# A decoder layer on one core: VectorE adds the negated maxima of 6 of 32 score tiles, 13 warm-up products, and all orders written anew

## What is computed

```python
# 1. linear attention, 16 heads of depth 8
q = elu(x @ Wq + bq) + 1 ; k = elu(x @ Wk + bk) + 1 ; v = x @ Wv + bv
k = k / sqrt(sum(k * k) + EPS)
attn = (q k^T) v @ Wo + bo
x = layernorm(x + (layernorm(x + attn) * gamma + beta))
# 2. cross attention to 64 context rows, 16 heads of 64
scores = (x @ Wq) (ctx @ Wk)^T / 8
out = softmax(scores) (ctx @ Wv) @ Wo
x = layernorm(x + out)
# 3. gated MLP, every operand rounded to FP4 in blocks of 16
h = silu(fp4(x) @ fp4(w_gate)^T) * (fp4(x) @ fp4(w_up)^T)      # 352 wide
x = layernorm(x + fp4(h) @ fp4(w_down)^T)
```

## Time and profile before

| | |
|---|---|
| median of 3 runs | 372.65 us |
| profiled execution, its own time | 374.35 us |
| its span | 372.6 us |
| PE, DVE, ACT, POOL busy | 351.0, 307.9, 253.4, 269.1 us |
| PE weight loads busy | 268.7 us |
| DMA | 10.44 MB, mean 28 GB/s |

### The profile page before, as it was taken

How to read it: one execution, slowest core, us unless ns; L and a number is a source line. 1 busy time by engine, 2 the same in 40 slices (tenths; PEclk the granted TensorE clock), 3 DMA queues, 4 the chain that set the end, 5 groups by cost and what they waited for, 6 DMA issues and landing times.

```text
span 372.6 us, 7321 instructions
## 1 busy us (share of the span) xinstructions
PE 351.0 (94%) x2143; PEld 268.7 (72%) x2143; DVE 307.9 (83%) x858; ACT 253.4 (68%) x533; POOL 269.1 (72%) x453
## 2 busy tenths in 40 slices
PE   7999998999998999999999999999999999998874
PEld 6688655775775968778678867786777788887663
DVE  2798756658689998869989779979998998999994
ACT  2757867586677678668687767868767656864553
POOL 4403549967988689969779895898989569784535
PEclk9999999999999999999999999999999999999998
DMA  7900100001000001000000000000000000000010
GB/s 251 300 2 16 30 1 14 16 16 29 15 17 14 2 15 43 16 30 17 15 29 14 17 1 17 28 3 0 17 15 2 15 2 0 8 23 14 3 30 28
DMA packets 13586, 10.44 MB, mean 28 GB/s; under 512 B 971, under 2 KB 12396, under 8 KB 13548
## 3 DMA queue, kind: packets, MB, share of 16 engines
q1 hardware_dynamic: 12540, 7.89, 7.0%
q10 hardware_dynamic: 1008, 2.10, 1.7%
HBM read 7.88 MB, written 2.10 MB: 27 GB/s over the span
## 4 chain that ended last, share of the span: by engine, by line
PE 71%; POOL 8%; DVE 8%; issue 6%; ACT 5%; DMA 1%; POOLq 0%; ACTq 0%; DVEq 0%
PE A L2860 13%; PE S L2833 12%; PE TP L2823 7%; PE F L2879 6%; PE TP L2851 6%; PE A L2895 5%; PE A L2784 3%; PE S L2842 3%; PE TP L2762 2%; POOL pe L431 2%; PE S L2762 2%; PE F L2762 2%; PE TP L2888 2%; PE A L2797 2%; DMA wqkT<-in_wk_t 1%
## 5 line engine op out<-in xcount | busy, mean ns | idle before, releaser
L431 POOL TENSOR_TENSOR pe<-pe,srec 128x1024 f32<-128x1024 f32 x32 | 60.9, 1904 | 9.2 <-DVE srec L1835 8.9
L2833 PE MATMUL S<-M,x1T 128*128 128x512 f32 x128 | 60.7, 597 | 1.5 <-ACT pe L1064 1.4
L2860 PEld LDWEIGHTS A<-wvoT,wqkT 128*128 128x128 f32 x480 | 56.4, 192 | 3.1 <-issue 1.8
L2860 PE MATMUL A<-wvoT,wqkT 128*128 128x128 f32 x480 | 58.0, 276 | 0.1
L425 POOL TENSOR_TENSOR fold<-pe 128x512 f32<-128x512 f32 x32 | 40.8, 1276 | 14.5 <-ACT pe L1064 14.2
L1818 DVE TENSOR_REDUCE smax<-S 128x16 fp32r<-128x1024 f32 x32 | 38.7, 1210 | 3.2 <-PE S L2833 3.1
L1064 ACT ACTIVATE pe<-S 128x1024 f32<-128x1024 f32 x32 | 32.6, 1020 | 10.6 <-PE S L2842 10.3
L1069 ACT ACTIVATE wqkT<-TP 128x1024 f32<-128x1024 f32 x32 | 32.6, 1019 | 4.3 <-PE TP L2851 4.1
L2833 PEld LDWEIGHTS S<-M,x1T 128*128 128x128 f32 x128 | 22.2, 190 | 18.3 <-issue 15.3
L2879 PE MATMUL F<-w_gu_r,xf_r 128*128 128x352 f32 x168 | 35.0, 344 | 0.1
L2851 PE MATMUL TP<-ident,pe 128*128 128x128 f32 x256 | 33.5, 274 | 1.6 <-POOL pe L431 1.0
(11 more groups left out here) (247 smaller groups left out, 890.2 us busy)
## 6 DMA issues: line engine op xcount, KB each, us to landing
xT<-in_x_t SPq DMA_DIRECT2D x16, 128.0 KB, 2.1
x_sb<-in_x SPq DMA_DIRECT2D x16, 128.0 KB, 2.1
out<-yf SPq DMA_DIRECT2D x15, 128.0 KB, 1.8
M<-in_fw SPq DMA_DIRECT2D x1, 560.0 KB, 11.0
wqkT<-in_wq_t ACTq DMA_DIRECT2D x2, 256.0 KB, 4.5
wqkT<-in_wk_t ACTq DMA_DIRECT2D x2, 256.0 KB, 5.8
ctx_f<-in_ctx_t ACTq DMA_DIRECT2D x2, 256.0 KB, 6.9
wvoT<-in_wv_t ACTq DMA_DIRECT2D x1, 512.0 KB, 9.2
```

The costliest lines, as they stand in the source:

```text
L431: ge.tensor_tensor(w, w, spread(srec[n % 2][:, :], HX, R), ALU.mult).then_inc(pn_made, 1)
L2833: last = te.matmul(S[:, half * BANK:half * BANK + BANK], x1T[b % 2][:, t * P:t * P + P], M[:, b // BH, HC * half:HC * half + HC, b % BH * ...
L2860: last = te.matmul(A2[:, t * P:t * P + P], pT[n % 2][:, j, :], vo[b % 2][:, j, :], start=(j == 0), stop=(j == NJ - 1))
```

## The change

There are four parts.

1. In the lists, `scores_shift` of tiles (1,1), (3,1), (5,1), (7,1), (9,1) and (11,1) stands in DVE's list and no longer in PE's. On DVE it is one addition of 128x1024 in place in PSUM.
2. `WARM` goes from 8 to 13, and the second group of `keep_warm` near the end from 14 to 19. The first of those two groups keeps its 7 products, writes to `F0` in place of `TP0` and stands one `gate_up` earlier.
3. All five lists are in a new order, SP's too.
4. Storage: `xf_r` lies in the tile `GT`, which is free once `m_product` is done; `xfT` has two buffers; the number of `fold`, `ssum` and `srec` buffers has a name (`NFO`), and it is 2 as before. New branches (`SUM_ON_PE`, `WHOLE_GATE`, `TILE_SUM_ON_PE`) are switched off: the sets are empty and the flag is False.

```diff
-        NXB, NA, NPE = 4, 5, 3
+        NXB, NA, NPE, NFO = 4, 5, 3, 2
...
-        xf_r = several("xf_r", 2, [P, 2, T * P], FP32R)
-        xfT = sb("xfT", [P, T * P])
+
+        xf_r = [GT[:, k, 0:2 * T, :].rearrange("p (s t) n -> p s (t n)", s=2) for k in range(2)]
+        xfT = several("xfT", 2, [P, T * P])
...
+        WHOLE_GATE = ()
+
+        SUM_ON_PE = ()
+
+        TILE_SUM_ON_PE = False
...
-        WARM = 8
+        WARM = 13
...
-                wait_free(pool, ssum_made, n - 1)
+                wait_free(pool, ssum_made, n - NFO + 1)
...
+                if b in SUM_ON_PE:
+                    pe.wait_ge(x1_made, T * b + T)
+                    te.matmul(part(A2, t), ident[:, :], x1[b % NA][:, t, :], start=True, stop=False)
...
```

More of the change, by code:

```diff
@@ L2875, in gate_up @@
                 pe.wait_ge(xfT_kept, b + 1)
+                if b in WHOLE_GATE:
+                    for m, bk in enumerate(ffn_banks(b)):
+                        last = te.matmul(bk[:, 0:I], part(xfT[b % 2], t), w_gu[:, m, :], start=True, stop=True)
+                    last.then_inc(gu_made, 1)
+                    return
                 pe.wait_ge(xf_low_made, b + 1)
@@ L3216, in _ @@
             pe.wait_ge(yx_made, 5)
+            down(0)
+            pe.wait_ge(vo_kept, 7)
+            p_transpose(5, 1)
+            pe.wait_ge(yf_made, 1)
             down(1)
@@ L3250, in _ @@
-            p_transpose(6, 0)
+            pe.wait_ge(h_made, 7)
+            gate_up(3, 1)
+            pe.wait_ge(fk_made, 11)
+            project_q(9)
             pe.wait_ge(ya_made, 9)
             kv_outer(9)
-            pe.wait_ge(h_made, 7)
-            gate_up(3, 1)
+            pe.wait_ge(pT_kept, 13)
+            p_transpose(6, 1)
+            kv_project(9)
+            pe.wait_ge(fq_made, 10)
+            down(2)
+            attn_out(9)
+            pe.wait_ge(yf_made, 3)
+            cross_out(6, 0)
@@ new lines, in _ @@
+            pe.wait_ge(yx_made, 9)
+            project_kv(13)
+            pe.wait_ge(pe_made, 20)
+            x1_transpose(10)
+            pe.wait_ge(pT_kept, 19)
+            values(10)
+            pe.wait_ge(fk_made, 14)
+            xf_transpose(6)
+            pe.wait_ge(x1T_kept, 11)
+            scores(10, 0)
+            pe.wait_ge(ky_made, 39)
+            kv_project(11)
+            pe.wait_ge(vo_kept, 11)
+            h_transpose(5)
+            pe.wait_ge(kvo_kept, 12)
+            kv_outer(12)
@@ L3381, in _ @@
+            pe.wait_ge(yf_made, 6)
+            xf_transpose(7)
+            pe.wait_ge(vo_kept, 12)
+            h_transpose(6)
+            pe.wait_ge(xf_low_made, 8)
+            project_q(11)
+            pe.wait_ge(hT_kept, 7)
+            p_transpose(10, 0)
+            pe.wait_ge(hg4_made, 7)
+            gate_up(7, 0)
+            pe.wait_ge(fq_made, 12)
+            down(6)
+            pe.wait_ge(ky_made, 42)
+            attn_out(11)
+            pe.wait_ge(yf_made, 7)
             project_q(12)
-            pe.wait_ge(xg_made, 9)
@@ new lines, in _ @@
+            xf_transpose(10)
+            pe.wait_ge(xg_made, 11)
+            kv_outer(15)
+            pe.wait_ge(hT_kept, 10)
+            values(14)
+            pe.wait_ge(xf_low_made, 11)
+            down(9)
+            pe.wait_ge(xg_made, 12)
+            kv_project(15)
+            pe.wait_ge(hg4_made, 10)
+            gate_up(10, 0)
+            attn_out(15)
+            pe.wait_ge(yf_made, 10)
+            xf_transpose(11)
+            pe.wait_ge(pe_made, 28)
+            x1_transpose(14)
```

2800 lines of the change are left out of this document (1393 added, 1407 removed).

## The result

The changed kernel takes 376.66 us (median of 4, 376.47 to 376.84) and the kernel before, run beside it, 372.65 us (372.3 to 372.77): ratio 1.0109, 95% interval 1.0092 to 1.0127. It is slower by 4.0 us; 369.4 was predicted, and the range ended at 374.5.

What follows compares the result with a forecast made beforehand. PE's list was taken to bound some 310 us, DVE's remaining work and the last tile's chain a 43 us tail. -3.1 + 1.2 - 1.4 + 0.3 - 0.3 = -3.3 from 374.35, less 1.70: 369.4 us, range 365.5 to 374.5.

Steps and rivals of the forecast that it cites:

- Six shifts off PE: Long stretch: six shifts at 0.51 us leave PE's list, -3.1 us (at most 4.1).
- six additions on DVE: Six tiles: 1.21 us each on DVE, S free 0.7 us later; 30% of 4.1 us taken, +1.2 us.
- The cover: Score tiles: PE's other products hide most of the later release of S; 30% of 4.1 us stays uncovered.
- the first rival: Long stretch: PE waits for all 7.3 us of added DVE work; +2.8 us, 375.5 us; chance 0.18.
- Work moved past the last scores: Ahead of scores(15, 1) PE has 1.4 us less work, so the last tile starts 1.4 us sooner: -1.4 us.
- The prediction's own mark: Long stretch, 120 to 320 us: the prediction is wrong if PE's idle time grows past 6 us.
- The third rival: 53.6 to 120 us: the new order also closes half of PE's 5.2 us idle time; 366.8 us; chance 0.18.
- The tail: After the last score maximum: later transposes, less DVE work after the last residual; +0.3 us, length stays 43 us.
- The warm-up and the start: Start: thirteen products close the gap before the weights, first products run at full clock; -0.3 us (-1.5 to +0.9).
- At nothing: Parts priced at zero: five more products near the end (0.12 us each), the storage changes, SP's list with store_out(2).
- DVE sets the pace: Long stretch: DVE goes to 92% busy and PE waits for all 7.3 us added; 375.5 us; chance 0.18.
- The score tile's path eats it: Score tiles: all 4.1 us of the later release of S fall on PE; no change, 372.3 us; chance 0.12.

Runs made afterwards that it cites:

- 13-product run: The kernel before with 13 warm-up products at the start in place of 8, nothing else: 372.56 us, ratio to before 0.9967.
- the filled wait: Changed kernel without its first tail warm-up group (375.1 us), with p_transpose(7,0) moved ahead of x1_transpose(8), which waited 1.35 us: 376.33 us.
- the one experiment on the rest of the tail: Changed kernel without its first tail warm-up group, with down(13) moved behind tile_gate_up(15,0) on PE alone: 377.69 us.
- the run with the new start: Changed lists up to tile (1,1), its shift on PE, 13 warm-up products and the new storage, then the lists of the kernel before: 373.39 us.
- the short sums: score_sums reads half its columns, in both orders: 376.68 us in the changed kernel, 373.86 in the kernel before (beside its 373.93).

## Why the prediction failed, step by step

*Six shifts off PE, and six additions on DVE* (-3.1 and +1.2): right, in the changed order. The addition was sized at 1.21 us and took 1.218. Together -1.9 us, measured -1.9; only the sum was measured. The cover was not the one that I named, though. I took 30% from PE's few waits; in the old order the same additions lose 4.3 us between the first maximum and the last, where -1.9 would have been a gain, so there the additions cost 4.3 + 3.1 = 7.4 us by my price of the shifts, the whole of their 7.3. That is the first rival's arithmetic, but not its reason: taking 6.4 us of other work off DVE gives nothing. What an addition delays is awaited, `S` at (3,1), a small result at (5,1) and (7,1), and only an order laid around it hides it.

*Work moved past the last scores* (-1.4): this is the step that failed. I counted PE's products ahead of the last `scores` and took for granted that the new order runs as tightly as the old one. With the shifts on PE the last maximum comes 2.6 us later than in the 13-product run, where I had it 1.4 earlier: 4.0 us off. The prediction's own mark was passed, PE's idle time in the long stretch went from 1.9 to 6.5 us. The named waits there are for `A` and `S`; that closing one doesn't help was shown once (the filled wait). But little of the 4.0 us is idle time: from 20 to 328 us it is 6.9 us with the shifts back on PE and 7.2 in the 13-product run. One can add up, for both traces and up to the last `scores`, the time from the start of each PE step to the start of the next, less the recorded idle time (an estimate, good to a few tenths, since some product rows are missing from a trace). What I had counted is there: `cross_out` and `h_transpose` take 3.1 us less and `gate_up` 1.6 more, together -1.5 where I had -1.4. But the same calls of `attn_out` take 1.3 us more, `down` and `scores` 0.8 each and `x1_transpose` 0.6, 3.6 us in all, to which 0.7 us of recorded idle time up to that point come; the changed kernel's trace shows the same four within 0.3 us. So the step that failed is the price of the calls that stayed: I put their change at nothing. Whether a call takes longer because of a short wait that the profile counts as busy or because of its new neighbours, no run separates.

The third rival's premise came true and more: between 53.6 and 120 us PE's idle time fell by 4.1 us of 5.2. The last maximum is late all the same.

*The tail* (+0.3, bounds -1.5 and +1.5): mis-sized, 3.0 us against the 13-product run, and past the 1.5 us that I had named as a mark too. I read the moved calls and never priced the first warm-up group at its new place: 1.6 us, shown by taking it out. The other 1.5 us lie on DVE between `h_max(14)` and `h_scaled(14)`, by the traces. I had DVE's list of the tail as a sum of work on either side of the last tile's residual, and not as an order of steps in front of sequence 14's rounding, on which the end waits. That is read and not tested, since the one experiment on the rest of the tail was confounded.

*The warm-up and the start* (-0.3): of little weight, and of a wrong frame. The 1.16 us product and the earlier third `m_product` (14.07, where I had 14.6) came as forecast, but I priced them against an execution with the low-clock start and then took off 1.70 us for the median, which already has the good start. Counted against the lower group the start brings nothing: the same order in front of the old lists is 0.8 us above the 13-product kernel (0.4 in the spans).

*At nothing*: of the five products at the end this holds by the trace. `h_transpose(14)` still waits 0.28 us for POOL behind the group, so the group is covered; only their size was wrong, since 19 products take 4.40 us, 0.23 each and not 0.12. The storage and the place of `store_out(2)` are in the run with the new start as well, and cost there, together with that start, 0.8 us at most. They were not tried singly.

The sum in measured terms: order 2.6, tail 2.9 to 3.0, additions -1.9, together 3.7 in the trace (374.9 - 371.2), 4.0 to 4.1 in the medians. Of the 7.3 us between 369.4 and 376.66, 4.0 are the order up to the last scores, 2.7 the tail, and 0.3 the gain of the start that the median already had; the last 0.3 lie between traces and medians. Of the rivals, *DVE sets the pace* came nearest in its number (375.5), by luck, since the loss has other terms. As a mechanism the short sums speak against it, and against the rule beside it: by the Trainium skill, Perfetto Trace Analysis, "Identifying the Most-Contended Engine", an engine's busy share tells how contended it is, and PE's headroom is judged by its weight loads. By these DVE at 84% against weight loads at 72% is the most contended engine; the trace has these shares, but 6.4 us less on that engine changed nothing. *The score tile's path eats it* was the mechanism of part of the old order's loss (the 1.76 us at (3,1)); in the new order the additions win 1.9 us over the shifts, so it isn't the reason there.

## What to carry to other kernels

Moving work between engines and reordering the lists are two changes, and each needs its own price: run the order without the move and the move without the order. The price of a step on an in-order engine is set by who awaits what stands behind it, not by the engine's busy share; a count of the calls ahead of a mark says when it could come, not when it does. Before a trace is used as the base of a sum, look whether its start is that of the median run.

## What the chip showed that I had not expected

Eight warm-up products followed by a gap before the weights are there don't fix the level at which the first real products run: in the old order they take 2.08 us in three traces (gaps of 1.29 to 1.34 us) and 1.16 in a fourth (1.15 us), and the run times of before part by some 1.4 us. In the new order a gap of 0.90 us gave 2.08 as well, so the length of the gap alone doesn't decide it. With thirteen products `g_product(0)` took 1.16 us in the traces of the 13-product kernel and of the changed one, and at most 1.27 in any other. In the tail a wait of 1.6 us on PE was followed by a granted clock of 0.72 over 6 us, which made 19 warm-up products 1.5 us longer. A wait of that length doesn't always do so: the one of 1.74 us in front of `gate_up(14, 1)` left its rows at 1.24 us in the run without the first warm-up group, and in the run with three additions moved they took 1.73, at a granted clock of 0.79 from 350 to 354 us.
